# Attention's first steps: later weight split, statistics on two engines, context spectra first

## The chip, the cores and the metric

The kernel is one program on one core of a Trainium2 chip. The metric is device time in microseconds of one execution; three executions of the kernel before took 3350.08, 3347.52 and 3346.3 us, median 3347.52. A core has five engines that run side by side and meet only at semaphores: PE (TensorE), DVE (VectorE), ACT (ScalarE), POOL (GpSimd) and SP (SyncE, which here only issues DMAs, in order).

## The reference, cut to what matters

Two layers over x of 16 batches x 256 positions x 2048 channels. The change lies in the first: an auto-correlation attention between the layer-normed x and a context, and the preparation of the next stage's weights, which runs beside it.

```python
m = jnp.mean(x, axis=-1, keepdims=True); v = jnp.var(x, axis=-1, keepdims=True)
Q = (x - m) / jnp.sqrt(v + 1e-5)            # K = V = ctx
qf, kf = jnp.fft.fft(q, axis=2), jnp.fft.fft(k, axis=2)
corr = jnp.fft.ifft(qf * jnp.conj(kf), axis=2).real
w, idx = jax.lax.top_k(corr.transpose(0, 1, 3, 2), 11); w = softmax(w)
out[l] += w[i] * v[min(idx[i] + l, L - 1)]  # for each of the 11
x = x + out
x = x + _L0_ffn_ref(_layernorm(x), W, ...)  # W: 2048 x 2048
```

## The kernel before, in words

`attention_phase` works on chunks of 512 channels, four to a batch (CH), 64 in all (LAST). The order of work is written out by hand: `steps` calls one `step(it, k)` per engine 73 times (8 to an `it`, and a tail of 9), and each part of the work has a lag in steps: `chunk(it, k, lag)` gives the chunk that a part works on in this step, or None. AFTER_CX = 4 is the lag of the context's load, AFTER_S = 5 that of normalizing x and of folding x and context (sum and difference of the two halves of time), AFTER_F = 6 that of the spectra and correlations, AFTER_T = 7 that of the top 11, AFTER_I = 8 that of the inverse transform. Each engine takes its parts of a step in the order in which its `step` names them.

Whole batches of x have their own calendar: `batch(it, k)` is a number in every fourth step. Batch b's x (2 MB) is loaded by SP in step 4b (before everything for b = 0), its sums are taken by ACT in steps 4b+1 and 4b+2 (`mean`, L507), its squares in 4b+2 and 4b+3 (`squares`, L527), DVE adds these up (`variance`, L624), ACT takes the root (L596), DVE inverts it (`scales`, L641, L644), and from step 4b+5 ACT normalizes a chunk a step (L469).

Beside it the 2048 x 2048 weights are split into an fp16 high and low part and summed by rows and columns, one 128 x 512 piece a step: loads in step h (L204, L205), ACT's scaling, high part and row sum in step h+1 (L478, L482, L587), POOL's low part in h+1 (L325), SP's store in h+2 (L211); ACT's last piece starts at 1154.6 us. In the tail SP stores the sums (L247, L249) and loads the next stage's first x (L256). An all-engine barrier ends the phase (ACT's first row behind it is L1178); the FFN stage reads the split weights.

Names in the profile: `x_first` is xn (two batches of x); `c_first` holds cx (context) and xe (folded x); `feat` is vl, the context's row 128 copied to all partitions, `att` and `v_last_twice` twice that row (L495); `ce` the folded context; `w_f` = wf, `w_rows` = wn, `w_parts` = wp; `prod_q` = pq. bx, by, bz, bu are PSUM banks: x spectrum and later correlations, key spectrum, value spectrum, inverse.

Of the kernel before, what the change touches and what calls it, by code (L numbers as in the profile page):

```python
# [23 lines left out]
ACT = mybir.ActivationFunctionType  # L24
AX = mybir.AxisListType
P = 128
# [42 lines left out]
def attention_phase(nc, x, ctx, xT, dft, x1, x1_squares, wT, w_rows, w_split, w_sums, w_cols, ctx_pairs, x_first, c_first, ident, vl, v_twice, last_squares, x_in2, c_in2, sums_out):  # L69
# [15 lines left out]
    MIRROR = ((P - 1, L), (0, L), (0, P), (P, L))  # L85
    AFTER_CX, AFTER_S, AFTER_F, AFTER_XT, AFTER_T, AFTER_I = 4, 5, 6, 7, 7, 8

    stack = ExitStack()
# [7 lines left out]
    with stack:  # L96
# [38 lines left out]
        consts_in = sem("consts_in")  # L135
        x_in = [sem(f"x_in{i}") for i in range(2)]
        vl_in = [sem(f"v_last_in{i}") for i in range(2)]
        ce_ok, vl2_ok, eo_ok, dc_ok = map(sem, ("c_folded", "v_last_twice", "c_odd", "k_mean_ok"))
# [47 lines left out]
        def _(sp):  # L186
            sp.dma_start(xn[0][:], x[0, :, :].rearrange("(t p) n -> p t n", p=P)).then_inc(x_in[0], 16)
            for tile, m in zip((m_e, m_o), dft[0:2]):
# [5 lines left out]
            def split_step(it, k):  # L194

                h = chunk(it, k, 0)
                if h is not None:
                    c, r = block_of(it, k, 0)
                    row = counted(sp, r * P)
                    if least(h, 2):  # L200
                        sp.wait_ge(w_lo, h - 1)
                        sp.wait_ge(w_summed, h - 1)
                    n, q = h // (D // BW), h % (D // BW)
                    sp.dma_start(wn[k % 2][:], w_rows[n * P:(n + 1) * P, q * BW:(q + 1) * BW]).then_inc(wn_in[k % 2], 16)  # L204
                    sp.dma_start(wf[k % 2][:], wT[bass.ds(row, P), c * BW:(c + 1) * BW]).then_inc(w_in[k % 2], 16)  # L205
                h = chunk(it, k, 2)
                if h is not None:
                    c, r = block_of(it, k, 2)
                    tile = counted(sp, r)
                    sp.wait_ge(w_lo, h + 1)  # L210
                    sp.dma_start(w_split[c, :, :, bass.ds(tile, 1), :, :].rearrange("j p k a n -> p j (k a n)"), wp[k % 2][:].rearrange("p j a n -> p j (a n)")).then_inc(w_out[k % 2], 16)  # L211

            def step(it, k):
# [25 lines left out]
                if h is not None:  # L239
# [4 lines left out]
                    sp.dma_start(x1[bass.ds(pair, 1), :, c * CT:(c + 1) * CT, bb % 2 * L:(bb % 2 + 1) * L].rearrange("a p j t -> p (a j) t"), xo[s][:]).then_inc(x1_out[s], 16)  # L244
                if it is ITS and k == 2:
                    sp.wait_ge(w_summed, LAST)
                    sp.dma_start(w_sums, wrow[:]).then_inc(w_sums_out, 16)  # L247
                    sp.wait_ge(w_scaled, LAST)
                    sp.dma_start(w_cols, wcol[:]).then_inc(w_sums_out, 16)  # L249
# [14 lines left out]
        def _(pool):  # L264
# [52 lines left out]
            def split_step(it, k):  # L317

                h = chunk(it, k, 1)
                if h is None:  # L320
                    return
                w = wf[(k - 1) % 2]
                pool.wait_ge(w_hi, h + 1)
                parts = wp[(k - 1) % 2]
                pool.tensor_tensor(parts[:, :, 1, :], w[:].rearrange("p (j n) -> p j n", n=P), parts[:, :, 0, :], ALU.subtract).then_inc(w_lo, 1)  # L325
# [39 lines left out]
            def step(it, k):  # L365
                inverse_sums(it, k)
                fold_x(it, k)
                split_step(it, k)
                spectrum_sum(it, k)
                fold_ctx(it, k)  # L370
                token_sums(it, k)
                if it is ITS and k == AFTER_F:
                    pool.wait_ge(const_set, 3)
                    pool.wait_ge(xe_ok, 2 * LAST)
                    pool.wait_ge(ce_ok, 2 * LAST)
                    pool.wait_ge(q_mm, LAST)
                    for n in range(len(c_in2)):
                        pool.dma_start(c_first[:, n, :], ctx_pairs[0, :, n, :]).then_inc(c_in2[n], 16)
# [5 lines left out]
        def _(pe):  # L384
            pe.wait_ge(consts_in, 16 * N_CONST)

            def folded(out, mats, src, done, first=0):
                for m in range(2):
                    mm = pe.matmul(out[:, m, :], mats[:, m, :], src[:, first if m == 0 else 1, :], start=True, stop=True)  # L389
                mm.then_inc(done, 1)  # L390

            def step(it, k):
                f = chunk(it, k, AFTER_F)
                g = chunk(it, k, AFTER_I)
                t = chunk(it, k, AFTER_T)
                if f is not None:
                    kk = k - AFTER_F
                    pe.wait_ge(xe_ok, 2 * (f + 1))
                    if least(f, 1):
                        pe.wait_ge(c_sb, 2 * f)  # L400
                    folded(bx, m_e, xe[kk % 2], q_mm)
                    pe.wait_ge(ce_ok, 2 * (f + 1))
# [8 lines left out]
                    elif f == 1:  # L411
                        pe.wait_ge(v_sb, 1)
                    folded(bz, m_o, ce[kk % 2], v_mm, 2)
                if g is not None:
                    s = (k - AFTER_I) % 2
# [40 lines left out]
        def _(act):  # L456
# [14 lines left out]
            def split_step(it, k):  # L471

                h = chunk(it, k, 1)
                if h is None:
                    return
                w = wf[(k - 1) % 2]
                act.wait_ge(w_in[(k - 1) % 2], 16 * (4 * it + (k - 1) // 2 + 1))
                act.activation(w[:], w[:], ACT.Copy, scale=W_SCALE, accum_out=wcol[:, h:h + 1] if isinstance(h, int) else wcol[:, bass.ds(h, 1)]).then_inc(w_scaled, 1)  # L478
                act.wait_ge(w_scaled, h + 1)
                if least(h, 2):  # L480
                    act.wait_ge(w_out[(k - 1) % 2], 16 * (4 * it + (k - 1) // 2))
                act.activation(wp[(k - 1) % 2][:, :, 0, :], w[:].rearrange("p (j n) -> p j n", n=P), ACT.Copy).then_inc(w_hi, 1)  # L482

# [13 lines left out]
            def mean(it, k, a):  # L497
# [5 lines left out]
                if a == 0:  # L503
                    act.wait_ge(x_in[slot], 16 * (it + (k - 1) // STEPS + 1))
                    if least(b, 1):
                        act.wait_ge(ln_mean, b)
                act.activation(xn[slot][:, a, :], xn[slot][:, a, :], ACT.Copy, accum_out=total[:, a:a + 1]).then_inc(ln_sum, 1)  # L507
                if a == TT - 1:
# [5 lines left out]
            def squares(it, k, a):  # L514

                b = batch(it, k - 2 - a)
                if b is None:
                    return
# [4 lines left out]
                for n in range(PIECES):  # L523
                    at = TT * PIECES * b + PIECES * a + n
                    if n or a or least(b, 1):
# [10 lines left out]
            def step(it, k):  # L536
# [3 lines left out]
                normalize(it, k)  # L540
                last_rows(it, k)
                split_step(it, k)
# [39 lines left out]
                squares(it, k, 0)  # L582
                h = chunk(it, k, 1)
                if h is not None:
                    w = wn[(k - 1) % 2]
                    act.wait_ge(wn_in[(k - 1) % 2], 16 * (h // 2 + 1))
                    act.activation(w[:], w[:], ACT.Copy, scale=W_SCALE, accum_out=wrow[:, h:h + 1]).then_inc(w_summed, 1)  # L587
# [20 lines left out]
        def _(dve):  # L608
# [7 lines left out]
            def variance(it, k):  # L616

                b = batch(it, k - 3)
                if b is None:
                    return  # L620
                dve.wait_ge(ln_sq, TT * PIECES * (b + 1))
                if least(b, 1):
# [23 lines left out]
            def step(it, k):  # L646
# [74 lines left out]
                if t is not None:  # L721
                    s = (k - AFTER_T) % 2
                    dve.wait_ge(we_mm, t + 1)
                    if least(t, 1):
                        dve.wait_ge(ze_sum, t)
                    products(by[:], kf[s], pe_, ze_mul)
            steps(step)
    nc.clear_and_free_semaphores(sems)
# [1807 lines left out]
```

## Time and profile before

| | |
|---|---|
| median of three runs | 3347.52 us |
| the profiled execution | 3344.23 us, its span 3342.4 us |
| busy: PE, DVE, ACT, POOL | 2989.7, 2740.3, 2266.7, 1587.3 us |
| attention phase | 0 to 1299 us |
| FFN stage and masks | 1299 to about 2900 us |
| last stages | to 3342 us, granted clock 0.82 on the mean |

Busy time of an engine is the union of its instructions; the time outside the span (1.83 us) is launch and end. Line numbers are those of the kernel before.

### The profile page before, as it was taken

How to read it: one execution, taken by the hardware profiler on the slowest of the kernel's cores; microseconds unless marked ns; L12 is line 12 of the kernel's file. 1: busy time of each engine (PE TensorE's matmuls, PEld its weight loads, DVE VectorE, ACT ScalarE, POOL GpSimd, SP SyncE). 2: the span in 40 equal slices, each digit the busy share in tenths (PEclk: the TensorE clock that was granted, in tenths of full speed). 3: DMA queues.
4: the chain of work that ended last, by engine and by line, in shares of the span. 5: the costliest groups of instructions: out<-in, count | busy, mean ns of one | idle time of the engine just before them, and what ended most of it. 6: DMA issues, size and time to landing. Idle time of an engine off the chain costs nothing. (4 is left out here: it accounts for less than half of the span.)

```text
span 3342.4 us, 46695 instructions
## 1 busy us (share of the span) xinstructions
PE 2989.7 (89%) x12946; PEld 1597.7 (48%) x12946; DVE 2740.3 (82%) x7143; ACT 2266.7 (68%) x5953; POOL 1587.3 (47%) x1165
## 2 busy tenths in 40 slices
PE   3999999999999996999999999999999999367786
PEld 1666666666666663444444444444444444222222
DVE  1999999999999995667968878796878879667776
ACT  6787888888888752755766758575775756376663
POOL 3898999989999882001212121111211220035665
PEclk9999999999999998999999999999999999578987
DMA  6455555554555425353745547373644735425543
GB/s 200 155 174 179 163 164 173 158 179 153 173 168 185 139 79 168 90 181 95 200 144 171 160 134 218 111 208 117 171 165 141 208 120 134 148 87 214 212 175 154
DMA packets 272022, 532.17 MB, mean 159 GB/s; under 512 B 32648, under 2 KB 132744, under 8 KB 248976
## 3 DMA queue, kind: packets, MB, share of 16 engines
q1 hardware_dynamic: 245584, 422.17, 39.8%
q10 hardware_dynamic: 15168, 71.34, 7.7%
q0 software_dynamic: 11008, 35.66, 3.1%
q8 instruction: 103, 1.69, 0.2%
q14 instruction: 159, 1.30, 0.1%
HBM read 401.07 MB, written 128.02 MB: 158 GB/s over the span
## 5 line engine op out<-in xcount | busy, mean ns | idle before, releaser
L1015 PE MATMUL acc<-xh,wq 128*128 128x512 f16 x4096 | 1204.5, 381 | 46.3 <-DVE x_first L1677 17.2
L1015 PE MATMUL acc<-xl,wq 128*128 128x512 f16 x2048 | 758.8, 380 | 0.0
L1243 ACT ACTIVATE unused<-c_first,minus_guess 128x256 bf16<-128x256 f32 x1024 | 505.2, 495 | 282.6 <-DVE minus_guess L1551 221.1
L1015 PEld LDWEIGHTS acc<-xh,wq 128*128 128x128 f16 x4096 | 399.9, 98 | 531.5 <-DVE x_first L1677 22.1
L944 POOL DMA_DIRECT2D c_first<-ctx_pairs x120 | 66.4, 554 | 859.3 <-DVE mk L1602 848.8
L1015 PEld LDWEIGHTS acc<-xl,wq 128*128 128x128 f16 x2048 | 200.8, 98 | 243.1 <-issue 2.5
L423 PEld LDWEIGHTS bu<-m_iz,zf 128*128 128x128 f32 x2048 | 282.4, 193 | 53.1 <-issue 39.0
L423 PE MATMUL bu<-m_iz,zf 128*128 128x128 f32 (+2 forms) x2048 | 297.0, 304 | 7.8 <-POOL zf L272 7.8
L442 PE MATMUL bx<-m_ic,pf 128*128 128x256 f32 x1024 | 238.7, 387 | 34.3 <-POOL pf L336 34.3
L442 PEld LDWEIGHTS bx<-m_ic,pf 128*128 128x128 f32 x1024 | 191.4, 192 | 69.0 <-POOL pf L336 45.0
L2136 PE MATMUL lw<-x,rt 128*66 128x512 f32 x256 | 142.9, 712 | 71.4 <-DVE x L2348 71.4
L272 POOL TENSOR_TENSOR zf<-prod_e 128x1024 f32<-128x1024 f32 x64 | 151.2, 2362 | 90.9 <-DVE prod_e L614 90.9
L1225 ACT ACTIVATE unread<-cf 128x256 bf16<-128x256 f32 x256 | 106.1, 414 | 127.3 <-DVE feat_pair L1650 99.3
L1243 ACT ACTIVATION_READ_ACCUMULATOR unused<-c_first,minus_guess 128x1 f32 x1024 | 191.5, 187 | 0.0
L2055 POOL TENSOR_TENSOR ost<-x,a 128x1024 f32<-128x1024 f32 x64 | 149.2, 2360 | 53.5 <-ACT a L2275 53.5
L336 POOL TENSOR_TENSOR pf<-prod_q 128x512 f32<-128x512 f32 x128 | 160.0, 1270 | 8.6 <-DVE prod_q L673 8.6
L389 PE MATMUL bx<-c_first,m_e 128*128 128x512 f32 x256 | 122.2, 600 | 37.6 <-POOL c_first L299 36.8
L272 POOL TENSOR_TENSOR zf<-prod_o 128x1024 f32<-128x1024 f32 x64 | 151.1, 2361 | 0.0
L2061 POOL TENSOR_TENSOR sq<-sq 128x1024 f32<-128x1024 f32 x32 | 75.2, 2350 | 155.9 <-ACT sq L2238 155.9
L957 POOL TENSOR_TENSOR x_first<-x_first,r 128x1024 f32<-128x1024 f32 x32 | 75.2, 2351 | 124.8 <-ACT r L1215 121.2
L550 ACT ACTIVATE kf<-by 128x512 f32<-128x512 f32 x64 | 38.2, 597 | 138.8 <-PE by L389 138.7
L2356 DVE SCALAR_TENSOR_TENSOR ost<-po,ost 128x512 f32<-128x512 f32 x128 | 81.0, 683 | 62.3 <-PE po L2129 51.7
(351 smaller groups left out, 7127.6 us busy)
## 6 DMA issues: line engine op xcount, KB each, us to landing
wq<-w_split SPq DMA_DIRECT2D x512, 256.0 KB, 3.1
x_first<-x SPq DMA_DIRECT2D x16, 2048.0 KB, 7.6
c_first<-ctx SPq DMA_DIRECT2D x64, 512.0 KB, 6.6
xt<-xT SPq DMA_DIRECT2D x64, 512.0 KB, 6.0
x_pairs<-xo SPq DMA_DIRECT2D x64, 512.0 KB, 3.2
c_first<-ctx_pairs POOLq DMA_DIRECT2D x128, 256.0 KB, 4.6
x<-xn_pairs SPq DMA_DIRECT2D x32, 1024.0 KB, 6.9
out_pairs<-ost SPq DMA_DIRECT2D x32, 1024.0 KB, 4.8
```

Source lines behind the costliest of these rows:

```text
L272: pool.tensor_tensor(out, v[:, :, 0, :], v[:, :, 1, :], ALU.add).then_inc(added, 1)
L336: pool.tensor_tensor(pf[(k - AFTER_F) % 2][:, a, :], pq[:, 2 * a, :], pq[:, 2 * a + 1, :], ALU.add).then_inc(p_sum, 1)
L389: mm = pe.matmul(out[:, m, :], mats[:, m, :], src[:, first if m == 0 else 1, :], start=True, stop=True)
L423: mm = pe.matmul(bu[:, j // 2, (j % 2) * L + c0:(j % 2) * L + c1], zf[s][:, a, j * P:(j + 1) * P], m_iz[:, a, c0:c1], start=a == 1 and j % ...
L442: mm = pe.matmul(bx[:, j // 2, (j % 2) * L:(j % 2 + 1) * L], pf[s][:, a, j * P:(j + 1) * P], m_ic[:, a, :], start=a == 0, stop=a == TT - 1)
L957: pool.tensor_tensor(v, v, r3[:].unsqueeze(1).broadcast_to([P, 2, T]), ALU.mult).then_inc(xn3_ok, 1)
L1015: return pe.matmul(acc[b][:], ws[(WQ * o + k // CK) % WR][:, k % CK, a, :], x[:, k, :], start=start, stop=False)
L1225: act.activation(unread[:, 0, :], cf[n % 4][:], ACT.Copy, accum_out=fp[:, 1, n % 2, n // 2:n // 2 + 1]).then_inc(csum_ok, 1)
L1243: act.activation(signs[:, u // 2, t] if n == COUNTS - 1 else unused[u % 2][:], ct[k % CR][:, t], ACT.Sign, bias=guess[q % 2][:, u:u + 1], ...
L2055: pool.tensor_tensor(ost[c][:, h % CH * HK:(h % CH + 1) * HK, :], xr[s][:, h * HK:(h + 1) * HK, :], a1[s][:].unsqueeze(1).broadcast_to([P, ...
L2136: pe.matmul(lw[0:A, :], rt[:, k, :], xr[s][:, k, :], start=k == 0, stop=False)
L2356: dve.scalar_tensor_tensor(o, po[(KT * s + k) % RING][:], DOWN, o, ALU.mult, ALU.add).then_inc(out_ok, 1)
```

## The change

The lag of the weights' split becomes a constant AFTER_W = 4, so piece h is loaded in step h+4, worked on in h+5 and stored in h+6; buffers are chosen by h instead of k, which is the same buffer. Batch 0's x comes in two DMAs with a semaphore each; ACT takes sum and squares of the first half, DVE those of the second, ahead of its steps, with `prod_q` as the place for the unused products. For chunk 0 alone the context's last row is doubled by ACT in step 2 instead of 5, POOL folds the context before x in step 5, and PE makes the key and value spectra before the x spectrum in step 6. In the tail the splitting goes on for four more steps, and the sums are stored in tail step 6 instead of 2. Nothing else of the program changes. The core of the diff:

```diff
+    AFTER_W = 4
...
+        x_second_in, ln_sq_second = sem("x_second_in"), sem("ln_sq_second")
...
-            sp.dma_start(xn[0][:], x[0, :, :].rearrange("(t p) n -> p t n", p=P)).then_inc(x_in[0], 16)
+            sp.dma_start(xn[0][:, 0, :], x[0, 0:P, :]).then_inc(x_in[0], 16)
+            sp.dma_start(xn[0][:, 1, :], x[0, P:L, :]).then_inc(x_second_in, 16)
...
-                h = chunk(it, k, 0)
...
                     if least(h, 2):
                         sp.wait_ge(w_lo, h - 1)
                         sp.wait_ge(w_summed, h - 1)
...
+                    sp.dma_start(wn[h % 2][:], w_rows[n * P:(n + 1) * P, q * BW:(q + 1) * BW]).then_inc(wn_in[h % 2], 16)
+                    sp.dma_start(wf[h % 2][:], wT[bass.ds(row, P), c * BW:(c + 1) * BW]).then_inc(w_in[h % 2], 16)
+                h = chunk(it, k, AFTER_W + 2)
...
-                    sp.dma_start(w_split[c, :, :, bass.ds(tile, 1), :, :].rearrange("j p k a n -> p j (k a n)"), wp[k % 2][:].rearrange("p j a n -> p j (a n)")).then_inc(w_out[k % 2], 16)
...
-                if it is ITS and k == 2:
+                if it is ITS and k == AFTER_W + 2:
...
-                h = chunk(it, k, 1)
...
-                w = wf[(k - 1) % 2]
+                w = wf[h % 2]
...
-                parts = wp[(k - 1) % 2]
+                parts = wp[h % 2]
...
             def step(it, k):
                 inverse_sums(it, k)
+                if it == 0 and k == AFTER_S:
+                    fold_ctx(it, k)
                 fold_x(it, k)
                 split_step(it, k)
                 spectrum_sum(it, k)
-                fold_ctx(it, k)
+                if it or k != AFTER_S:
+                    fold_ctx(it, k)
...
+            def spectrum_of_x(f):
+                pe.wait_ge(xe_ok, 2 * (f + 1))
+                if least(f, 1):
+                    pe.wait_ge(c_sb, 2 * f)
+                folded(bx, m_e, xe[f % 2], q_mm)
...
                 if f is not None:
                     kk = k - AFTER_F
-                    pe.wait_ge(xe_ok, 2 * (f + 1))
                     if least(f, 1):
-                        pe.wait_ge(c_sb, 2 * f)
-                    folded(bx, m_e, xe[kk % 2], q_mm)
+                        spectrum_of_x(f)
...
                     folded(bz, m_o, ce[kk % 2], v_mm, 2)
+                    if not least(f, 1):
+                        spectrum_of_x(f)
...
-                h = chunk(it, k, 1)
...
-                w = wf[(k - 1) % 2]
-                act.wait_ge(w_in[(k - 1) % 2], 16 * (4 * it + (k - 1) // 2 + 1))
+                w = wf[h % 2]
+                act.wait_ge(w_in[h % 2], 16 * (h // 2 + 1))
...
-                    act.wait_ge(w_out[(k - 1) % 2], 16 * (4 * it + (k - 1) // 2))
-                act.activation(wp[(k - 1) % 2][:, :, 0, :], w[:].rearrange("p (j n) -> p j n", n=P), ACT.Copy).then_inc(w_hi, 1)
+                    act.wait_ge(w_out[h % 2], 16 * (h // 2))
...
-                act.activation(xn[slot][:, a, :], xn[slot][:, a, :], ACT.Copy, accum_out=total[:, a:a + 1]).then_inc(ln_sum, 1)
+                if a == 0 or b:
+                    act.activation(xn[slot][:, a, :], xn[slot][:, a, :], ACT.Copy, accum_out=total[:, a:a + 1]).then_inc(ln_sum, 1)
...
                 b = batch(it, k - 2 - a)
-                if b is None:
+                if b is None or (a and not b):
...
-                    at = TT * PIECES * b + PIECES * a + n
+                    at = TT * PIECES * b + PIECES * a + n - (PIECES if b else 0)
...
-                last_rows(it, k)
+                if it or k != AFTER_S:
+                    last_rows(it, k)
+                if it == 0 and k == 2:
+                    last_rows(it, AFTER_S)
...
-                h = chunk(it, k, 1)
...
-                dve.wait_ge(ln_sq, TT * PIECES * (b + 1))
+                dve.wait_ge(ln_sq, TT * PIECES * (b + 1) - PIECES)
+                dve.wait_ge(ln_sq_second, PIECES)
...
+            second = xn[0][:, 1, :]
+            dve.wait_ge(x_second_in, 16)
+            dve.tensor_reduce(total[:, 1:2], second, AX.X, ALU.add).then_inc(ln_sum, 1)
+            dve.wait_ge(ln_mean, 1)
+            for n in range(PIECES):
+                half = second[:, n * D // PIECES:(n + 1) * D // PIECES]
+                unused = pq[:].rearrange("p c n -> p (c n)")[:, n * D // PIECES:(n + 1) * D // PIECES]
+                dve.scalar_tensor_tensor(unused, half, negative[:, 1:2], half, ALU.add, ALU.mult, accum_out=parts[:, 1, n:n + 1]).then_inc(ln_sq_second, 1)
             steps(step)
```

ACT's queue from batch 0's first squares to the first normalized chunk, before (two pieces of split and both sums of x stand ahead of it):

```order
L527 ACTIVATE unread_squares,var_parts<-x_first,minus_mean 128x1024 x2
L587 ACTIVATE w_rows,w_row_sums<-w_rows 128x512
L478 ACTIVATE w_f_0,w_cols_sb<-w_f_0 128x512
L482 ACTIVATE w_parts<-w_f_0 128x4x128
L527 ACTIVATE unread_squares,var_parts<-x_first,minus_mean 128x1024 x2
L587 ACTIVATE w_rows,w_row_sums<-w_rows 128x512
L596 ACT_TABLE_LOAD
L596 ACTIVATE std<-var,eps 128x2
L478 ACTIVATE w_f_1,w_cols_sb<-w_f_1 128x512
L482 ACTIVATE w_parts<-w_f_1 128x4x128
L587 ACTIVATE w_rows,w_row_sums<-w_rows 128x512
L469 ACTIVATE x_first<-x_first,nmr,rstd 128x512 x2
```

and of the change, from the phase's very first work to the sum of batch 1's first half:

```order
L520 ACTIVATE x_first,x_total<-x_first 128x2048
L507 ACTIVATE att<-feat 128x512
L525 ACTIVATE minus_mean<-x_total 128x2
L540 ACTIVATE unread_squares,var_parts<-x_first,minus_mean 128x1024 x2
L612 ACT_TABLE_LOAD
L612 ACTIVATE std<-var,eps 128x2
L481 ACTIVATE x_first<-x_first,nmr,rstd 128x512 x2
L490 ACTIVATE w_f_0,w_cols_sb<-w_f_0 128x512
L494 ACTIVATE w_parts<-w_f_0 128x4x128
L520 ACTIVATE x_first,x_total<-x_first 128x2048
```

Four pieces of split (w_f, w_parts, w_rows) stand no longer ahead of the first normalization, the first of them has moved behind it; the doubled row (`att<-feat`) has moved ahead of `minus_mean`; one `x_first,x_total` and one pair of squares are gone.

SP's queue of DMAs, before, from the third piece of weights to batch 1's x; each pair of weight loads and each store waits for ACT or POOL:

```order
L204 DMA w_rows<-w_rows 128x512
L205 DMA w_f_0<-wT 128x512
L211 DMA w_split<-w_parts 128x4x256
L204 DMA w_rows<-w_rows 128x512
L205 DMA w_f_1<-wT 128x512
L211 DMA w_split<-w_parts 128x4x256
L204 DMA w_rows<-w_rows 128x512
L205 DMA w_f_0<-wT 128x512
L211 DMA w_split<-w_parts 128x4x256
L224 DMA feat<-ctx 128x512
L225 DMA c_first<-ctx 128x2x512
L237 DMA x_first<-x 128x2x2048
```

and of the change, from the last constant on; none of these rows waits:

```order
L195 DMA ident<-identity 128x128
L207 DMA w_rows<-w_rows 128x512
L208 DMA w_f_0<-wT 128x512
L227 DMA feat<-ctx 128x512
L228 DMA c_first<-ctx 128x2x512
L240 DMA x_first<-x 128x2x2048
L207 DMA w_rows<-w_rows 128x512
L208 DMA w_f_1<-wT 128x512
L227 DMA feat<-ctx 128x512
L228 DMA c_first<-ctx 128x2x512
```

The rows of ctx (`feat`, `c_first`) and the second batch of x now stand right behind one piece of weights, ahead of every row that waits for ACT or POOL.

DVE's queue of the change, from its start to the first product of spectra:

```order
L746 TENSOR_REDUCE x_total<-x_first 128x1
L751 SCALAR_TENSOR_TENSOR prod_q,var_parts<-x_first,minus_mean 128x1024 x2
L641 TENSOR_REDUCE var<-var_parts 128x2
L658 RECIPROCAL rstd<-std 128x2
L661 TENSOR_SCALAR nmr<-minus_mean,rstd 128x1 x2
L685 SCALAR_TENSOR_TENSOR kf<-att,by 1x512
L690 TENSOR_TENSOR prod_q<-bx,kf 128x1024
```

The first two rows are new; the others stood at the head of DVE's queue before.

## Rows read from the trace of the kernel before

**Rows 1.** Stretches: bounds, length, busy of PE PEld DVE ACT POOL, clock, DMA share, GB/s
```profile
60.00:1300.00 1240.00, 1138.94 (x4844) 764.21 (x4842) 1149.76 (x2617) 947.00 (x1727) 1080.44 (x839) 0.99 0.52 161
...
2900.00:3342.40 442.40, 316.04 (x868) 112.00 (x868) 325.30 (x536) 246.31 (x378) 225.78 (x104) 0.82 0.47 175
```
**Rows 2.** The timeline's start: start us, us, engine line op out<-in, idle before
```profile
13.19 1.28 ACT L478 ACT_TABLE_LOAD   x1 [13.19 <-DMA w_f<-wT]
...
21.57 0.20 ACT L512 ACTIVATE minus_mean<-x_total 128x2 f32<-128x2 f32 x1
...
21.80 1.15 ACT L527 ACTIVATE unread_squares<-x_first,minus_mean 128x1024 bf16<-128x1024 f32 x1
...
24.22 0.61 ACT L587 ACTIVATE w_rows<-w_rows 128x512 f32<-128x512 f32 x1
...
29.23 1.28 ACT L596 ACT_TABLE_LOAD   x1
...
30.53 0.30 ACT L596 ACTIVATE std<-var,eps 128x2 f32<-128x2 f32 x1
...
31.06 0.33 DVE L644 TENSOR_SCALAR nmr<-minus_mean,rstd 128x1 f32<-128x1 f32 x2
...
31.69 0.55 SPq L237 DMA_DIRECT2D x_first<-x  x1
...
36.83 3.75 PE L389 MATMUL bx<-c_first,m_e 128*128 128x512 f32 x4 [36.83 <-POOL c_first L299]
...
42.77 1.91 ACT L507 ACTIVATE x_first<-x_first 128x2048 f32<-128x2048 f32 x1 [4.95 <-DMA x_first<-x]
...
45.29 1.51 ACT L469 ACTIVATE x_first<-x_first,nmr,rstd 128x512 f32<-128x512 f32 x2
...
46.70 0.62 ACT L495 ACTIVATE v_last_twice<-feat 128x512 f32<-128x512 f32 x1
...
47.22 0.61 ACT L478 ACTIVATE w_f<-w_f 128x512 f32<-128x512 f32 x1
...
48.50 1.89 ACT L507 ACTIVATE x_first<-x_first 128x2048 f32<-128x2048 f32 x1
...
50.74 0.60 ACT L550 ACTIVATE kf<-by 128x512 f32<-128x512 f32 x1
```
**Rows 3.** DMA issues, each asked in its own short stretch: KB, us to landing
```profile
x_first<-x SPq DMA_DIRECT2D x1, 2048.0 KB, 7.7
...
ident<-identity SPq DMA_DIRECT2D x1, 64.0 KB, 8.3
...
w_rows<-w_rows SPq DMA_DIRECT2D x1, 256.0 KB, 7.1
...
feat<-ctx SPq DMA_DIRECT2D x1, 256.0 KB, 5.3
...
x_first<-x SPq DMA_DIRECT2D x1, 2048.0 KB, 11.1
c_first<-ctx SPq DMA_DIRECT2D x1, 512.0 KB, 6.6
```
**Rows 4.** DVE groups by form: count, busy us, mean ns, idle before
```profile
L2310 DVE SCALAR_TENSOR_TENSOR ost<-ost,cw 128x256 f32<-128x256 f32 x26 | 10.4, 480 | 0.0
...
L1433 DVE SCALAR_TENSOR_TENSOR aug_a<-xr,aug_a 64x2048 f16<-64x2048 f32 x1 | 2.3, 2291 | 0.0
...
L1401 DVE TENSOR_REDUCE lora_sum<-xr 64x1 f32<-64x2048 f32 x1 | 2.3, 2271 | 0.0
```
**Rows 5.** Stretches of one step each in steady work and tail, columns as in Rows 1
```profile
1101.02:1119.31 18.29, 17.33 (x76) 11.54 (x75) 17.49 (x40) 15.99 (x29) 16.70 (x14) 1.00 0.47 144
...
1194.88:1213.17 18.29, 17.80 (x78) 11.86 (x77) 17.85 (x42) 10.70 (x20) 16.08 (x13) 1.00 0.37 105
```
**Rows 6.** Line L256, the next stage's x: us from issue to landing
```profile
DMA to landing us min/median/max: 5.9/10.1/14.5
```
**Rows 7.** The timeline at the phase's end, ACT
```profile
1299.39 1.91 ACT L1178 ACTIVATE xh<-x_first 128x2048 f16<-128x2048 f32 x1 [7.70 <-PEq L729]
```

More of the change, by code:

```diff
@@ L194, in split_step @@
             def split_step(it, k):
-                h = chunk(it, k, 0)
+                h = chunk(it, k, AFTER_W)
                 if h is not None:
-                    c, r = block_of(it, k, 0)
+                    c, r = block_of(it, k, AFTER_W)
                     row = counted(sp, r * P)
@@ L203, in split_step @@
                     n, q = h // (D // BW), h % (D // BW)
-                    sp.dma_start(wn[k % 2][:], w_rows[n * P:(n + 1) * P, q * BW:(q + 1) * BW]).then_inc(wn_in[k % 2], 16)
-                    sp.dma_start(wf[k % 2][:], wT[bass.ds(row, P), c * BW:(c + 1) * BW]).then_inc(w_in[k % 2], 16)
-                h = chunk(it, k, 2)
+                    sp.dma_start(wn[h % 2][:], w_rows[n * P:(n + 1) * P, q * BW:(q + 1) * BW]).then_inc(wn_in[h % 2], 16)
+                    sp.dma_start(wf[h % 2][:], wT[bass.ds(row, P), c * BW:(c + 1) * BW]).then_inc(w_in[h % 2], 16)
+                h = chunk(it, k, AFTER_W + 2)
                 if h is not None:
-                    c, r = block_of(it, k, 2)
+                    c, r = block_of(it, k, AFTER_W + 2)
                     tile = counted(sp, r)
                     sp.wait_ge(w_lo, h + 1)
-                    sp.dma_start(w_split[c, :, :, bass.ds(tile, 1), :, :].rearrange("j p k a n -> p j (k a n)"), wp[k % 2][:].rearrange("p j a n -> p j (a n)")).then_inc(w_out[k % 2], 16)
+                    sp.dma_start(w_split[c, :, :, bass.ds(tile, 1), :, :].rearrange("j p k a n -> p j (k a n)"), wp[h % 2][:].rearrange("p j a n -> p j (a n)")).then_inc(w_out[h % 2], 16)
             def step(it, k):
@@ L317, in split_step @@
             def split_step(it, k):
-                h = chunk(it, k, 1)
+                h = chunk(it, k, AFTER_W + 1)
                 if h is None:
                     return
-                w = wf[(k - 1) % 2]
+                w = wf[h % 2]
                 pool.wait_ge(w_hi, h + 1)
-                parts = wp[(k - 1) % 2]
+                parts = wp[h % 2]
                 pool.tensor_tensor(parts[:, :, 1, :], w[:].rearrange("p (j n) -> p j n", n=P), parts[:, :, 0, :], ALU.subtract).then_inc(w_lo, 1)
@@ L471, in split_step @@
             def split_step(it, k):
-                h = chunk(it, k, 1)
+                h = chunk(it, k, AFTER_W + 1)
                 if h is None:
                     return
-                w = wf[(k - 1) % 2]
-                act.wait_ge(w_in[(k - 1) % 2], 16 * (4 * it + (k - 1) // 2 + 1))
+                w = wf[h % 2]
+                act.wait_ge(w_in[h % 2], 16 * (h // 2 + 1))
                 act.activation(w[:], w[:], ACT.Copy, scale=W_SCALE, accum_out=wcol[:, h:h + 1] if isinstance(h, int) else wcol[:, bass.ds(h, 1)]).then_inc(w_scaled, 1)
@@ L480, in split_step @@
                 if least(h, 2):
-                    act.wait_ge(w_out[(k - 1) % 2], 16 * (4 * it + (k - 1) // 2))
-                act.activation(wp[(k - 1) % 2][:, :, 0, :], w[:].rearrange("p (j n) -> p j n", n=P), ACT.Copy).then_inc(w_hi, 1)
+                    act.wait_ge(w_out[h % 2], 16 * (h // 2))
+                act.activation(wp[h % 2][:, :, 0, :], w[:].rearrange("p (j n) -> p j n", n=P), ACT.Copy).then_inc(w_hi, 1)
             def last_rows(it, k):
@@ L582, in step @@
                 squares(it, k, 0)
-                h = chunk(it, k, 1)
+                h = chunk(it, k, AFTER_W + 1)
                 if h is not None:
-                    w = wn[(k - 1) % 2]
-                    act.wait_ge(wn_in[(k - 1) % 2], 16 * (h // 2 + 1))
+                    w = wn[h % 2]
+                    act.wait_ge(wn_in[h % 2], 16 * (h // 2 + 1))
                     act.activation(w[:], w[:], ACT.Copy, scale=W_SCALE, accum_out=wrow[:, h:h + 1]).then_inc(w_summed, 1)
```

## The prediction

> **What bounds the kernel now.** I read the stretches first, then the timeline of the start, then the steps at the attention phase's end. From 60 to 1300 us DVE is busy 1149.76 of 1240 us and PE 1138.94 [rows 1]: the steady part runs at the pace of DVE with PE close behind. The first 60 us are different. ACT does nothing until 13.19 us, when its first row is released by the landing of w_f, a piece of weights, though batch 0's x had landed at 0.76 + 7.7 = 8.46 us (its issue is the phase's first) [rows 2, 3]. Then ACT alone is the path: sums, squares, four pieces of split and a table load, with the root at 30.53 and the scale factors done at 31.39. PE makes its first spectrum at 36.83. At 42.77 ACT comes out of an idle stretch of 4.95 us that batch 1's x ended; this load was issued at 31.69 [rows 2, 3], since in SP's queue it stood behind loads and stores that wait for ACT and POOL. From 42.77 to the first copy of a key spectrum (L550) at 50.74, ACT has no gap [rows 2]; that is 7.97 us of its own work. L550 is where I measure: the order behind it is the same in both kernels.
>
> **The start, step by step.** DMAs of this start land in the order of issue. ident, the last constant, was issued at 3.51 and lands at 3.51 + 8.3 = 11.8 us, the second w_rows, issued at 6.70, at 6.70 + 7.1 = 13.80 [rows 3]. In the change the third DMA behind ident is no longer that one but the context row (feat), which has the same 256 KB; the split of x in two adds an issue but no byte. So I put its landing at 13.80 too.
>
> ACT: the first half of x lands at the latest with the whole at 8.46; table load 1.28, sum 1.89 and its read 0.2 end by 11.9, so this is hidden behind the feat row with 1.9 us to spare. Where it really lands (sooner by about half the transfer) doesn't matter. Then `att<-feat` 0.52 to the next start (46.70 to 47.22) gives 14.32. minus_mean also waits for DVE's sum of the second half. DVE starts when the constants are in, 11.8, and the nearest row for 2048 columns is L1401 with 2.27 us [rows 4], so it ends at 14.1, 0.2 before ACT is there. If the 128-partition form took twice the 64-partition one, it would be 16.4 and cost 2.0; I take 2.27 because every other form here goes by columns.
>
> minus_mean to squares 0.23 (21.57 to 21.80), two squares 2.42 (21.80 to 24.22): ACT is free at 17.0. The table load for the root then takes 1.30 to the next start (29.23 to 30.53): 18.3. In before 24.22 to 29.23, one split piece, two squares and a row sum, lay between. Meanwhile DVE has two STT instructions of 1024 columns with an accumulator. Not one row shows this form. From 480 ns at 256 and 2291 at 2048 columns [rows 4] a straight line gives 1.26 us; two of them with reads of some 0.1 end at 14.55 + 2.7 = 17.3, and the variance (below 0.2) at 17.5. That lies under the table load with 0.8 us to spare. The far end is L1433's 2.29 each: 19.3, variance 19.5, which costs 1.2 us. Lower end: nothing gained, as the table load is in front. I take the line.
>
> The Trainium skill speaks against this edit: Vector Engine (DVE) Microarchitecture Reference, section "Points that are easy to get wrong", says that a scalar_tensor_tensor with two non-bf16 SBUF sources runs at half throughput, because both read ports are taken. L2310 is such an instruction without an accumulator, and at 480 ns for 256 columns [rows 4] it doesn't show this; no row has it with one. By that rule the sum would be the far end above, 1.2 us worse.
>
> Root to scale factors 0.86 (30.53 to 31.39): 19.2. Normalizing chunk 0 takes 1.41 to the next start (45.29 to 46.70) and the split piece 1.28 (47.22 to 48.50), which ACT now does before it looks at batch 1's x: 21.9. Is that x there? It stands behind feat and the context chunk. In before, these three, issued half a microsecond apart, landed at 30.61 + 5.3 = 35.9, 31.16 + 6.6 = 37.8 and 31.69 + 11.1 = 42.8 [rows 3], so 1.9 and 5.0 us apart: 13.8 + 6.9 = 20.7, 1.2 us before ACT asks. Then ACT's 7.97 us run follows as before and L550 starts at 29.9 instead of 50.74. **The lead is 20.8 us.** Its other inputs: by and bz need only the context, long there. bx came 5.4 us after the scale factors (31.39 to 36.83), with ACT and POOL work between; even so it starts at 24.6 and is through by 29, and its reader on DVE stands behind L550. The next piece of weights and context row land within 2 to 3 us of 20.7 and are asked for at about 26. PE's clock at the start is not on the path.
>
> **What is added later.** From step 6 to 64 the queues do the same work a step as before, and nothing there reads a clock; the lead stays whole. In steps 65 to 69 ACT, POOL and SP still have pieces of split, where before the last was at 1154.6. A steady step with its piece and part of the statistics has ACT busy 15.99 us, a tail step 10.70, and both take 18.29 [rows 5]: ACT's extra 1.28 + 0.62 us and POOL's are hidden behind DVE. Cost 0, at most 5 x 1.9 = 9.5 if none were. SP's two stores of sums now stand ahead of the next stage's x in its queue: two issues, under 2 us later, and the x, issued from 1270.2 on and landed 14.5 us later at most (by 1286.7), is first read at 1299.39 [rows 6, 7]. Hidden by over 10 us.
>
> **The sum.** 50.74 - 29.9 = 20.8, less 0.3 for semaphore hops that I haven't counted one by one: 20.5 us. The profiled execution took 3344.23 us, so its like would take 3323.7; the median of the runs, 3347.52, is 3.3 above it, and I predict that: **3327.0 us**.
>
> **Rivals.**
> (1) *Batch 1's x, not ACT, sets L550.* Four more DMAs are issued behind this x at once (w_rows, w_f, feat, c_first: 1280 KB), where before ACT's pace spread them. If they share the engines with it instead of queueing, x lands with the last of them: 2048 KB took 5.0 us, so 1280 KB 3.1 us, landing at 23.8, 1.9 us after ACT asks. For it: the order of DMAs is no promise. Against: each landing of the first 14 us comes in order of issue. Together with the slow STT it is 3.1 us: 3330. The Trainium skill has the rule (DMA: Bandwidth & Descriptors, "Queues, rings and completion order": a later descriptor may finish before an earlier one, completion is not first-in first-out per issuing engine). By the landings so far the trace doesn't show it.
> (2) *The tail takes some back.* The slack of DVE's 18.29 us in the tail isn't that of the steady steps. All of ACT's extra: 9.5 us, 3336.5. Against it stand the equal pitches [rows 5].
> (3) *The start isn't what carries.* If some later transfer or the barrier at 1299 had slack of 20 us, the lead would be waited out: 3347.5. Against it: from 60 to 1300 us PE and DVE are idle for 101 and 90 us in all, under 2 us a step on the mean [rows 1], so there is little to wait out in.
> (4) *Slower: the clock of the last stages.* From 2900 us on, PE is granted 0.82 of its 2.4 GHz on the mean, so it is at its lower level of 1.2 GHz for some 36% of 442 us, about 160 us [rows 1]. Nothing in that stage is changed, but it starts 20.5 us sooner, and a level is set by what PE did before. At the lower level work takes twice as long, so each us of work moved there costs one. It decides from the point at which 20.5 us of PE's work more is done at 1.2 GHz; with 30 us the time is 3356. Against it: the three runs lie within 3.8 us, so the levels fall alike each time.
>
> **Numbers.** Forecast 76 in 100; (1) 13; (2) 4; (3) 4; (4) 3. About 0.2%, 6.7 us, is what a measurement of this kernel can tell from no change. The first three cases are all faster by more: faster 0.93, same 0.04, slower 0.03. The range: the forecast's own unknowns are +3.2 (STT and sum of the second half), the runs' spread -1.2 to +2.6, and a lead up to 1.5 larger if feat lands sooner. I take 3323.5 to 3332, which leaves out (2) in full, (3) and (4).
>
> **What would show it.** In the profile after: ACT's `att<-feat` starts near 13.8 after an idle stretch that the DMA feat ended; the table load for the root near 17.0 and the root near 18.3, without a wait for DVE; batch 1's sum near 21.9 without a wait for its x; L550 near 29.9; DVE's pitch in steady steps and steps 65 to 69 at 18.29; xh (L1178's counterpart) at 1278.9. A root that waits for DVE's var shows slow STTs; an idle stretch before batch 1's sum shows rival 1; a PEclk below 0.82 in the last 440 us shows rival 4. I am wrong if L550 leads by 20 us and xh doesn't.

## The result, and the profile after

The change takes 3329.48 us (median of five executions, 3325.17 to 3331.88), the kernel before on the same chip 3347.32 us (3345.15 to 3350.08): ratio 0.9946, 95% interval 0.9936 to 0.9957, so 17.84 us faster. The forecast was 3327.0 us, in a range from 3323.5 to 3332.0. Line numbers below are those of each kernel's own program; the change's L520 is L507 of before, L540 is L527, L612 is L596, L566 is L550.

ACT in the change, from its first work on (start us, us, engine line, operation, out<-in, and in brackets the idle time before it and what ended it):

```profile
5.71 1.28 ACT L520 ACT_TABLE_LOAD   x1 [5.71 <-DMA x_first<-x]
7.00 1.91 ACT L520 ACTIVATE x_first<-x_first 128x2048 f32<-128x2048 f32 x1
...
15.07 0.63 ACT L507 ACTIVATE att<-feat 128x512 f32<-128x512 f32 x1 [6.07 <-DMA feat<-ctx]
15.61 0.19 ACT L525 ACTIVATE minus_mean<-x_total 128x2 f32<-128x2 f32 x1
15.82 1.15 ACT L540 ACTIVATE unread_squares<-x_first,minus_mean 128x1024 bf16<-128x1024 f32 x1
...
18.36 1.28 ACT L612 ACT_TABLE_LOAD   x1
19.65 0.29 ACT L612 ACTIVATE std<-var,eps 128x2 f32<-128x2 f32 x1
20.55 1.52 ACT L481 ACTIVATE x_first<-x_first,nmr,rstd 128x512 f32<-128x512 f32 x2 [0.60 <-DVE nmr L661]
21.98 0.61 ACT L490 ACTIVATE w_f<-w_f 128x512 f32<-128x512 f32 x1
...
23.25 1.89 ACT L520 ACTIVATE x_first<-x_first 128x2048 f32<-128x2048 f32 x1
...
31.20 0.60 ACT L566 ACTIVATE kf<-by 128x512 f32<-128x512 f32 x1
```

Against [rows 2]: the root's table load is at 18.36 instead of 29.23, and batch 1's sum at 23.25 has no wait, where at 42.77 it had waited 4.95. The first key copy stands at 31.20 instead of 50.74, a lead of 19.54 us. The one long wait that is left is the 6.07 us for feat, behind the sum of x's first half (over at 9.01).

DVE and POOL beside it:

```profile
11.65 2.29 DVE L746 TENSOR_REDUCE x_total<-x_first 128x1 f32<-128x2048 f32 x1 [11.65 <-DMA ident<-identity]
15.83 1.29 DVE L751 SCALAR_TENSOR_TENSOR prod_q<-x_first,minus_mean 128x1024 f32<-128x1024 f32 x1 [1.89 <-ACT minus_mean L525]
...
17.04 2.28 DVE L751 SCALAR_TENSOR_TENSOR prod_q<-x_first,minus_mean 128x1024 f32<-128x1024 f32 x1
...
19.43 0.16 DVE L641 TENSOR_REDUCE var<-var_parts 128x2 f32<-128x4 f32 x1
```
```profile
16.78 1.46 POOL L314 TENSOR_TENSOR ce<-c_first 128x512 f32<-128x512 f32 x1 [15.75 <-DMA c_first<-ctx]
18.20 2.24 POOL L315 TENSOR_TENSOR ce<-c_first 128x512 f32<-128x512 f32 x1
```

These are two equal instructions of DVE, 1.29 and 2.28 us. The second runs beside POOL's two adds, which take 1.46 and 2.24. The variance is ready at 19.59, just ahead of the root at 19.65.

Three of the DMAs issued between 5.9 and 9 us (KB, us from issue to landing):

```profile
x_first<-x SPq DMA_DIRECT2D x1, 2048.0 KB, 13.7
...
w_f<-wT SPq DMA_DIRECT2D x1, 256.0 KB, 7.0
feat<-ctx SPq DMA_DIRECT2D x1, 256.0 KB, 8.6
```

w_f was issued at 5.92 and landed at 12.9, feat at 6.46 and landed at 15.05: 2.1 us apart for the same 256 KB. Batch 1's x was issued at 8.08 and landed at 21.8.

The stretches, as in [rows 1] (the attention phase from 60 us on, the FFN stage, the last stages), and one tail step, as in [rows 5]:

```profile
60.00:1281.77 1221.77, 1128.72 (x4813) 757.97 (x4811) 1140.62 (x2587) 938.81 (x1720) 1074.04 (x819) 0.99 0.52 164
1281.77:2885.00 1603.23, 1525.44 (x7214) 717.86 (x7214) 1262.58 (x3983) 1037.00 (x3782) 259.80 (x214) 0.98 0.52 151
2885.00:3327.60 442.60, 313.32 (x868) 111.04 (x868) 325.32 (x536) 246.32 (x378) 225.82 (x104) 0.83 0.47 175
...
1177.04:1195.80 18.76, 17.80 (x78) 11.97 (x77) 17.96 (x42) 12.51 (x24) 17.17 (x14) 1.00 0.52 140
```

xh starts at 1281.77 instead of 1299.39 [rows 7], a lead of 17.62 us. The last stages have the busy times of before within 3 us, at a granted clock of 0.83 against 0.82. The tail step took 18.76 us where the tail step of before took 18.29 [rows 5].

### The profile page after: what moved, and what is told of

The parts are those of the page before. It is cut to its first block and busy times, and to the rows that moved or that the text cites. A ratio compares the mean times of both kernels' runs of the same rounds, so it can differ in the third digit from the quotient of the medians.

```text
span 3327.7 us, 46695 instructions
## 1 busy us (share of the span) xinstructions
PE 2989.0 (90%) x12946; PEld 1599.5 (48%) x12946; DVE 2748.3 (83%) x7148; ACT 2262.8 (68%) x5947; POOL 1588.3 (48%) x1165
## 5 line engine op out<-in xcount | busy, mean ns | idle before, releaser
L395 PE MATMUL by<-ce,m_e 128*128 128x512 f32 x256 | 122.0, 599 | 20.6 <-POOL ce L315 20.6
L2254 ACT ACTIVATE gc<-mk,att 128x256 f32<-128x256 uint8 x256 | 128.7, 587 | 2.1 <-DVE att L2357 2.1
```

The source lines that it names most:

```text
L2254: g = act.activation(gc[c][:, k - c * CK, t], mk[s][:, k, t], ACT.Identity, bias=att[:, 1, k % 2, bass.ds(b, 1), k // 2], scale=att[:, 0, ...
```

## The experiments

Each time is a median beside runs of the kernel before on the same chip: 3347.63 us beside the first four, 3345.03 beside the next four, 3346.03 beside the last.

**The split alone.** Second and third part undone:

```diff
-            sp.dma_start(xn[0][:, 0, :], x[0, 0:P, :]).then_inc(x_in[0], 16)
-            sp.dma_start(xn[0][:, 1, :], x[0, P:L, :]).then_inc(x_second_in, 16)
+            sp.dma_start(xn[0][:], x[0, :, :].rearrange("(t p) n -> p t n", p=P)).then_inc(x_in[0], 16)
...
-            second = xn[0][:, 1, :]
...
```

> The change's later split alone; batch 0's statistics all on ACT and the old order of context and spectra. My theory: the late split carries nearly all of the lead, since it frees ACT before the root and lets batch 1's x be issued with the first loads. From rows of both kernels: x in at 8.4, table load 1.3, two sums 3.7 and minus_mean 0.2 to 13.7, four squares 4.85 to 18.5, table load and root to 20.7 for the scale factors, normalize 1.4, doubled row 0.5, split 1.3: batch 1's sum at 23.9 against 23.25 with all three parts, so L550's copy 0.7 later than the change's 31.20, at 31.9; lead over before 18.9, whole time 17 us under before. Rival: the two engines for the statistics and the early context carry a third or more of the lead; then L550 stands at 37 or later and the time is at most 12 us under before.

3332.29 us, ratio 0.9955 (0.9938 to 0.9972). The key copy (expected at 31.9) is at 32.74, a lead of 18.0, xh at 1284.06 (lead 15.33), and the tail's pitch, the time from one step to the next, is 18.76. So the split carries nearly all of the lead, and the tail's loss comes with it. It does two things at once: it takes four pieces out of ACT's way, and it lets batch 1's x be issued early. No run has one without the other, so their shares stay open.

**The statistics alone.** AFTER_W = 0, and the third part (the context's order) undone too, so that of the change only the second half's statistics on DVE are left. The line for the split:

```diff
-    AFTER_W = 4
+    AFTER_W = 0
```

> Batch 0's second half on DVE alone, the split at its old place, the old order of context and spectra. My theory: only ACT's own saving shows, one sum (1.9) and one pair of squares (2.4), 4.3 us, since batch 1's x is issued behind waits on ACT: L550 near 46.4, time 4 us under before. Rival: the statistics are the bottleneck of the start: L550 near 38, time 12 us under before.

3343.69 us, ratio 0.9991 (0.9981 to 1.0): hardly to be told from no change. The lead at the key copy is 3.82, at xh 2.81. Batch 1's x still sets the pace, since its load stands behind SP's waits. The rows are ACT's sum of it and the key copy:

```profile
38.95 1.91 ACT L514 ACTIVATE x_first<-x_first 128x2048 f32<-128x2048 f32 x1 [4.40 <-DMA x_first<-x]
...
46.92 0.60 ACT L557 ACTIVATE kf<-by 128x512 f32<-128x512 f32 x1
```

The tail's pitch is 18.29 again in all five steps.

**What costs time in the tail?** Both ACT and POOL have a piece of split there that they hadn't before. One kernel moves POOL's subtraction behind the spectrum sums, the other ACT's row sum to the end of its step, and a third does both.

```diff
                 fold_x(it, k)
-                split_step(it, k)
                 spectrum_sum(it, k)
+                split_step(it, k)
```

> The change, with POOL's low part of the split behind its two spectrum sums in every step instead of ahead of them. My theory: in steps 65 to 69 the change has a pitch of 18.77 where before had 18.29, since POOL's 1.16 us subtraction holds back the sums of products, and with them PE's correlations and the next spectra that DVE waits for; and the same 0.48 is hidden in the mean of the steady steps, 18.90. So the pitch falls to 18.29 in steps 65 to 69 and by up to 0.48 in the mean of four steady steps: up to 60 x 0.48 = 29 us, time near 3302. Rival: ACT's row sum between its copy of the inverse and that of the weights' spectrum sets it: no pitch changes, time as the change's, 3329. Second rival: POOL's later work (context fold, token sums) is late in turn: pitch 18.77 stays or rises.

> The change, with ACT's row sum of the weights (0.8 us) moved from ahead of its copy of the transposed weights' spectrum to the end of its step. My theory (POOL's subtraction is what costs): steps 65 to 69 keep 18.77, time within 3 us of the change's 3329. Rival (ACT's row sum costs): they fall to 18.29 and the steady mean with them, up to 29 us less.

> The change with both orders of e3 and e4: POOL's low part of the split behind the spectrum sums, ACT's row sum at the end of the step. With POOL's order alone two of four steady steps are at 18.29 and two at 18.75 and 19.32, in which batch statistics run. My theory: in these two ACT is late in front of its copy of the transposed weights' spectrum, and the row sum's 0.8 us stands right there, so it is hidden only once POOL's part is out of the way: both fall by up to 0.47, steady mean 18.43, another 13 us, time 3300. Rival: they are held by something else (table loads, statistics themselves, PE), and the row sum at the end only delays the next step's normalizing: mean 18.67 or more, time 3313 or more.

POOL's order: 3313.10 us, ratio 0.9895 (0.9879 to 0.9912), xh at 1266.56. ACT's: 3330.29 us, ratio 0.9946 (0.993 to 0.9963), the change's own. Both: 3303.81 us, ratio 0.9874 (0.9858 to 0.9891), xh at 1257.52. The mean of 56 steady steps is 18.901 us in before, 18.909 in the change, 18.667 with POOL's order, 18.912 with ACT's, 18.545 with both. One tail step of each of the three, in the order in which they are named here:

```profile
1162.26:1180.54 18.28, 17.80 (x78) 11.85 (x77) 17.83 (x41) 12.56 (x25) 17.18 (x14) 1.00 0.53 143
```
```profile
1177.04:1195.81 18.77, 17.81 (x78) 11.98 (x77) 17.97 (x42) 12.53 (x24) 17.17 (x14) 1.00 0.51 140
```
```profile
1156.11:1174.39 18.28, 17.80 (x78) 11.86 (x77) 17.83 (x41) 12.56 (x25) 17.14 (x14) 1.00 0.53 143
```

All have the same work (ACT busy 12.5, POOL 17.1 to 17.2), and only the order of POOL's queue decides between 18.28 and 18.77. How it does so is seen in POOL's rows, first of the change in that tail step, then with POOL's order:

```profile
1183.36 2.37 POOL L275 TENSOR_TENSOR zf<-prod_e 128x1024 f32<-128x1024 f32 x1 [1.29 <-DVE prod_e L630]
...
1190.46 1.17 POOL L328 TENSOR_TENSOR w_parts<-w_f,w_parts 128x512 f16<-128x512 f32 x1
1191.59 2.51 POOL L339 TENSOR_TENSOR pf<-prod_q 128x512 f32<-128x512 f32 x2
```
```profile
1168.11 2.37 POOL L275 TENSOR_TENSOR zf<-prod_e 128x1024 f32<-128x1024 f32 x1 [0.80 <-DVE prod_e L630]
...
1175.21 2.52 POOL L339 TENSOR_TENSOR pf<-prod_q 128x512 f32<-128x512 f32 x2
1177.66 1.19 POOL L328 TENSOR_TENSOR w_parts<-w_f,w_parts 128x512 f16<-128x512 f32 x1
```

pf starts 8.23 us behind zf in the one, 7.10 in the other; the difference is the subtraction. PE's inverse correlations (bx from m_ic and pf) read pf, and in that step of the change they wait for it:

```profile
1194.15 3.72 PE L454 MATMUL bx<-m_ic,pf 128*128 128x256 f32 x16 [0.59 <-POOL pf L339]
```

PE's waits from 120 to 1180 us (engine line, waited for: us in total, times, longest), in before and then with POOL's order:

```profile
PE by L434 <- DVE wk L680: 38.3, 56, 1.6
PE bx L442 <- POOL pf L336: 24.5, 41, 0.6
```
```profile
PE by L446 <- DVE wk L697: 39.3, 57, 1.7
PE by L395 <- DVE w_fold L727: 7.6, 13, 0.6
```

The wait for pf was in the kernel before, 41 times in 56 steps, and goes with the new order (in the change: 25.1 us, 42 times, so it isn't new there). With both orders the 7.6 us for w_fold are gone too. In the mid phase the cycle of four steps is 18.29, 19.22, 18.31, 19.78 in before, 18.29, 18.75, 18.30, 19.32 with POOL's order and 18.29, 18.29, 18.29, 19.31 with both. The expectations of 3302 us for POOL's order and 3300 for both were too low: POOL's order alone leaves two of four steps above 18.29, and with both orders the fourth keeps 1.02 us, for which no run has the cause.

**Feat ahead of the constants.** The row is issued right behind x, and DVE's wait for the constants stands behind its statistics:

```diff
             sp.dma_start(xn[0][:, 1, :], x[0, P:L, :]).then_inc(x_second_in, 16)
+            sp.dma_start(vl[0][:], ctx[0:1, L // 2, 0:CW].rearrange("a n -> (a n)").partition_broadcast(P)).then_inc(vl_in[0], 16)
...
-            dve.wait_ge(consts_in, 16 * N_CONST)
             second = xn[0][:, 1, :]
...
+            dve.wait_ge(consts_in, 16 * N_CONST)
```

> The change with chunk 0's context row (feat) issued right behind the two halves of x, ahead of the constants, and DVE waiting for the constants only behind its statistics. My theory: the row, which landed at 15.05, is what ACT waits 6.07 us for, and behind it the next limit is batch 1's x, which lands near 21.7 whatever ACT does. So minus_mean falls from 15.61 to about 11, the scale factors are done at about 16, batch 1's sum then waits for its x until 21.7, and L550 stands at 29.7 against 31.20: 1.5 us. Rival: batch 1's x lands sooner too, or no wait is left, and all 4.6 us come through: L550 at 26.6.

One execution, 3328.42 us. ACT:

```profile
10.15 0.63 ACT L509 ACTIVATE att<-feat 128x512 f32<-128x512 f32 x1 [0.96 <-DMA feat<-ctx]
...
21.82 1.91 ACT L522 ACTIVATE x_first<-x_first 128x2048 f32<-128x2048 f32 x1 [3.40 <-DMA x_first<-x]
...
29.79 0.60 ACT L568 ACTIVATE kf<-by 128x512 f32<-128x512 f32 x1
```

The statistics are 4.9 us sooner, and 3.4 of these are waited out for batch 1's x. That is the wait of rival 1, reached because ACT is early and not because the x is late. xh at 1280.79 is 0.98 us ahead of the change's.

**POOL's context fold after the statistics.** One wait more:

```diff
+                    pool.wait_ge(ln_sq_second, PIECES)
                     fold_ctx(it, k)
```

> The change with POOL's fold of chunk 0's context put off until DVE has done its two squares. In the change DVE's second scalar_tensor_tensor took 2.28 us against 1.29 for the first, while POOL's fold took 1.46 and 2.24 in place of 1.26. My theory: the two engines slow each other where both read their operands from SBUF. Then both of DVE's take 1.29, POOL's take 1.26, and L550 doesn't move by more than 0.1, since the table load hides DVE. Rival: the slow one is slow by itself (two f32 SBUF sources and the accumulator): it stays at 2.28.

One execution, 3329.07 us. DVE and POOL:

```profile
16.94 1.28 DVE L752 SCALAR_TENSOR_TENSOR prod_q<-x_first,minus_mean 128x1024 f32<-128x1024 f32 x1
```
```profile
18.31 1.26 POOL L314 TENSOR_TENSOR ce<-c_first 128x512 f32<-128x512 f32 x1 [17.27 <-DVE prod_q L752]
19.53 1.26 POOL L315 TENSOR_TENSOR ce<-c_first 128x512 f32<-128x512 f32 x1
```

Apart, they take 1.28 and 1.26 us; the slowing was mutual. The change's rows fit a taking of turns. By an estimate from them, with each instruction's own length counted back from its end, POOL's first add runs from 16.98 (DVE's first one ends at 17.12), DVE's second from 18.04 (that add ends at 18.24) and POOL's second add from 19.18 (DVE's second ends at 19.32). The key copy is at 31.11 against 31.20, so it had cost nothing behind the table load.

**The third part undone** (the context's order; split and statistics stay):

```diff
-                if it == 0 and k == AFTER_S:
-                    fold_ctx(it, k)
...
-                if it or k != AFTER_S:
-                    last_rows(it, k)
-                if it == 0 and k == 2:
-                    last_rows(it, AFTER_S)
+                last_rows(it, k)
```

> The change without its third part: chunk 0's context row is doubled in step 5 again, POOL folds x first, PE makes the x spectrum first. My theory: this part costs time, since it puts the wait for the row ahead of minus_mean: DVE's sum is done at 13.95, minus_mean then stands at 14.0 and not at 15.61, normalizing starts at 19.0 and not at 20.55, and the doubled row's 0.5 us comes behind it; L550 at 30.1 against 31.20, 1.1 us sooner. Rival: the early key spectrum is needed: ACT then waits at L550 for PE, which stands behind POOL's late fold, and L550 is at 31.2 or later.

One execution, 3323.4 us:

```profile
14.12 0.20 ACT L519 ACTIVATE minus_mean<-x_total 128x2 f32<-128x2 f32 x1 [5.06 <-DVE x_total L737]
...
30.25 0.60 ACT L557 ACTIVATE kf<-by 128x512 f32<-128x512 f32 x1
```

minus_mean no longer stands behind feat's row, and the key copy is 0.95 us sooner than in the change. But the first fold of weights on DVE (w_fold) is at 59.14 against 59.08, and xh at 1282.16 against 1281.77. At xh the third part is worth 0.4 us, no more than such single profiles scatter. At the key copy the three parts come to 18.0 for the split, 2.49 for the statistics on top of it (32.74 to 30.25), and 0.95 lost by the context's order. The 6 us by which this execution is shorter lie behind xh (below) and say nothing of it.

**Both orders and feat first, together**

> This kernel joins two edits measured apart: POOL's split piece behind the spectrum sum and ACT's row sum at the end of its step (3303.81 us together), and the context's first row issued right behind x with DVE's wait for the constants moved behind its statistics. The latter put the first key copy at 29.79 instead of 31.20 and xh 0.98 us sooner (1280.79 against 1281.77). Theory 'the two are independent': the key copy at 29.8, where ACT's wait of 3.4 us for batch 1's x is the new bound, the first pitches 21.56, the steady mean 18.545, xh near 1257.52 - 1.0 = 1256.5, and a median near 3302.8, which may be too little to tell from 3303.81. Theory 'the early lead gets lost in the first steps, since there PE and POOL set the pace': key copy at 29.8 but first w_fold no sooner than 59.45, xh at 1257.5.

3304.29 us (3300.87 to 3307.98), ratio 0.9877 (0.986 to 0.9893): the same as both orders alone. The key copy came 1.47 us sooner, at 29.82, the first w_fold at 59.37 against 59.45, and the first pitch was 22.26 against 21.56, so that from there on this kernel is 0.6 us behind. xh, at 1261.27, fits neither theory. Most of it is the phase's last step (between the last two folds of weights), which took 19.79 us where it took 16.97 with both orders alone. The stretch of this one step, first with both orders, then with feat first too, then of before and of the change:

```profile
1210.97:1227.94 16.97, 10.42 (x54) 7.27 (x52) 14.90 (x38) 4.84 (x10) 7.38 (x5) 1.00 0.19 62
```
```profile
1211.65:1231.44 19.79, 13.25 (x54) 9.58 (x52) 14.90 (x39) 4.84 (x10) 7.38 (x5) 0.83 0.18 53
```
```profile
1249.75:1269.59 19.84, 13.29 (x54) 9.62 (x52) 14.91 (x39) 4.83 (x10) 7.37 (x5) 0.83 0.16 53
```
```profile
1233.31:1251.96 18.65, 12.11 (x54) 8.62 (x52) 14.91 (x38) 4.84 (x10) 7.38 (x5) 0.91 0.19 57
```

DVE, ACT and POOL are busy for the same time in all four; only PE's time differs, with the granted clock. The other seven profiles agree: POOL's order has 19.59 us at 0.83, and six have 18.35 to 18.65 us at 0.91, among them the statistics alone, whose tail has no split. So up to 3 us of a single profile's lead at xh are PE's level in this one step, and no run shows what sets it there.

## Why the prediction was right, and where it wasn't

The time came out as forecast, and so did the mechanism of the start; four terms did not, and since they have both signs, the total is nearer than the terms are.

**Feat's landing: a size.** 13.80 was forecast, it was 15.05, since the row took 2.1 us behind w_f instead of the 0.7 that a 256 KB piece takes in the same queue. The assumption "same KB, same time" failed: this DMA copies one row of 2 KB to 128 partitions. The trace of before had a sign of it: feat landed at 35.9 and w_f, issued at 29.66 with 4.2 us to landing, at 33.9, 2.0 us apart, though with a store between them. All of ACT's start lies 1.25 later for it, and this is nearly the whole difference between the forecast 29.9 and the measured 31.20. The hidden first half (ACT idle from 9.01 on), 14.32 for minus_mean (15.61), 17.0 to 18.3 for the table load (18.36 to 19.65) and the 8.0 us from batch 1's sum to the key copy (7.95) hold once this is added.

**DVE's statistics: right with thin cover.** 2.27 forecast for the sum, 2.29 measured; 1.26 for each STT, 1.29 for the first. The second reached the far end (2.29 forecast, 2.28 measured), but by another way, POOL's adds beside it. It cost nothing, but the variance ended only 0.06 us ahead of the root. The rule of the Trainium skill (Vector Engine (DVE) Microarchitecture Reference, "Points that are easy to get wrong": half throughput with two non-bf16 SBUF sources) isn't borne out: with POOL held back both take 1.28 us for 1024 columns, no more a column than the sum, which has one source (2.29 us for 2048). The slow one is explained without it.

**Batch 1's x (rival 1): not in the change.** It landed at 21.8, 1.5 us before ACT asked; 20.7 was forecast. With ACT 4.9 us further ahead (feat first) it became the bound. The two pieces of weights issued right behind it landed after it, at 22.4 and 23.1. The rule that later descriptors may overtake (the Trainium skill, DMA: Bandwidth & Descriptors, "Queues, rings and completion order") shows in no landing that the trace has of this start: they come in order of issue.

**"Nothing there reads a clock; the lead stays whole": wrong by 1.2 us.** Of 19.54 us at the key copy 18.32 are left ahead of the tail. 0.5 goes by the first correlations on PE, which take 5.63 us at a granted clock of 0.65 where before took 5.11 at 0.72, and 0.26 in the first pitch (22.01 against 21.75, clock 0.95 against 0.96). 0.3 is lost in one step of the mid phase (20.09 us where before has 19.79), at a granted clock of 1.00 in both, so the clock isn't the cause there and it stays open. The rest is hundredths a step.

**The tail at "cost 0": the failed step.** From the equal pitches of [rows 5] I concluded that the split is hidden, and I named 18.29 for steps 65 to 69. The steady step that I took is one of the two short ones in a cycle of four (18.29, 19.22, 18.31, 19.78, mean 18.90). All four have the split, so two of them were above 18.29 with it, and nothing said on which side a tail step would fall. With the split a tail step takes 18.76 and loses 0.47; over four steps that is 1.9 us, near the low end of rival 2 (0 to 9.5). The experiments give the cause, which wasn't ACT's 1.9 us, as I had priced it, but POOL's 1.16 us ahead of pf. The last step gave 1.2 back (18.65 against 19.84), at a granted clock of 0.91 against 0.83. I hadn't forecast that, and the statistics alone have it too (18.43 at 0.91), so it is luck.

**The sum.** 20.5 forecast; measured 19.54 at the key copy, minus 1.2, minus 1.9, plus 1.2 gives 17.6 at xh, and the medians are 17.84 apart. The forecast time is 2.5 us low: the lead was overrated by 2.7.

**Two figures that don't follow from their own terms.** Rival 1 with slow STTs was put at 3.1 us, 3330. But slow STTs let ACT ask for x 1.2 us later, and x lands at 23.8 all the same, so the two together cost 1.9 us by these terms: 3328.9. In rival 4, 30 us in place of a gain give 3357 and not 3356. Neither case came up.

**Rivals 3 and 4.** Nothing waited the lead out: the leads at xh of the change, the split alone, the statistics alone, POOL's order and both orders (17.62, 15.33, 2.81, 32.83, 41.87) are carried into the medians (17.84, 15.34, 3.94, 34.53, 41.22). The last stages' clock is 0.83 against 0.82.

## What to carry to other kernels

Work moved from a start into a steady phase or a tail is hidden only where the queue that takes it isn't about to release an engine that others wait for. Look for who waits for that queue (here the 24.5 us of PE for POOL's pf, which stood in the profile of before), not at busy shares or one step's length. Where a wait of this kind shows, put the work that nobody waits for behind the one that is waited for: two such moves were worth 23 us here (41.22 less 17.84), more than the change; the second, ACT's, brought something only once the first was made. Compare steps over a whole cycle of the schedule.

## What the runs showed of the hardware

- DVE's scalar_tensor_tensor on 128x1024 f32 from SBUF takes 1.28 us alone and 2.28 beside two tensor_tensor of POOL from SBUF, which go from 1.26 each to 1.46 and 2.24. The three starts and ends fit turns taken between the engines.
- A DMA that copies a 2 KB row to 128 partitions (256 KB) landed 2.1 us behind its forerunner in the change, and 1.8 in the kernel that issues it right behind x (8.3 to 10.1); a 256 KB piece of weights 0.7.
- The phase's last step took 16.97 us at a granted clock of 1.00, 18.35 to 18.65 at 0.91 and 19.59 to 19.84 at 0.83, over eleven profiles.
- The time behind xh, where nothing differs, was 2043.0 us in before's profile, 2045.9 in the change's, and from 2039.4 to 2049.1 in the experiments'. A span of one profile thus can't tell 5 us. The lead at a milestone can, if the milestone lies ahead of the last step.
